# Causal attention: queries made and turned by heads, the first pairs before the last queries, VectorE's row work ahead of the inversion

## What is computed

```python
q = (x @ Wq).reshape(b, t, H, D)                  # H = 16 heads, D = 64: 32 plain, 32 to be turned
ckv = x @ Wkva                                    # 16 latent columns, 32 key columns to be turned
kv_latent, k_rope = ckv[:, :, :R], ckv[:, :, R:]
q = concat([q_nope, rope(q_rope)]); k = concat([kv, rope(k_rope)]); v = concat([kv, 0])
att = softmax(where(tril, q @ k.T / sqrt(D), -inf))   # 512 x 512, causal
y = (att @ v) @ Wo
```

## Time and profile before

| | us |
|---|---|
| median of three runs | 1535.96 (1533.09 to 1536.89) |
| the profiled execution | 1537.09 |
| its span, first to last instruction | 1535.1 |
| TensorE busy in the span | 1282.3 (84%) |
| VectorE, ScalarE, GpSimd busy | 949.6, 718.9, 531.6 |
| the causal attention in the span | 818.6 to 1172.3 |
| its exponentials of the first unit | at 849.1 |

### The profile page before, as it was taken

One profiled execution on the slowest core, in us unless ns is written; L12 is line 12 of the kernel. 1 busy time (PEld: TensorE's weight loads), 2 busy tenths in 40 slices (PEclk: granted clock), 3 DMA queues, 4 the chain that ended last, 5 costly groups with the idle time before them and its releaser, 6 DMA issues. The chain is left out here.

```text
span 1535.1 us, 25211 instructions
## 1 busy us (share of the span) xinstructions
PE 1282.3 (84%) x8930; PEld 743.7 (48%) x8930; DVE 949.6 (62%) x2159; ACT 718.9 (47%) x1936; POOL 531.6 (35%) x625
## 2 busy tenths in 40 slices
PE   3799718879999969958995889898987968987998
PEld 2444306745565636644433556564654434443443
DVE  6466631255756764566655788888664855665764
ACT  3254503367666524434442665656673333453222
POOL 2320250445433544341002565657452320001443
PEclk8599959989999979968996999999997986998999
DMA  2355021151000013230000000000000010000000
GB/s 57 108 168 128 25 69 39 41 119 15 1 1 1 8 60 108 56 65 9 11 2 1 1 1 1 1 1 1 1 1 1 1 22 13 10 3 1 7 7 14
DMA packets 67134, 45.31 MB, mean 30 GB/s; under 512 B 17707, under 2 KB 60403, under 8 KB 67011
## 3 DMA queue, kind: packets, MB, share of 16 engines
q1 hardware_dynamic: 61155, 34.48, 8.8%
q0 software_dynamic: 4096, 8.40, 2.3%
q10 hardware_dynamic: 1760, 0.82, 0.3%
HBM read 24.91 MB, written 13.89 MB: 25 GB/s over the span
## 5 line engine op out<-in xcount | busy, mean ns | idle before, releaser
L3479 ACT ACTIVATE L2a_pr<-psum,L2a_negmax 128x512 f32<-128x512 f32 (+3 forms) x256 | 132.2, 531 | 94.8 <-DVE L2a_negmax L3605 40.2
L585 ACT ACTIVATE L1x_praw<-psum,L1x_negmax 128x154 f32<-128x154 f32 x256 | 96.1, 390 | 56.9 <-DVE L1x_negmax L710 56.8
L3344 PE MATMUL psum<-ident,L2a_pr 128*128 128x128 f32 x640 | 86.6, 280 | 20.3 <-DVE L2a_pT L3618 12.9
L319 POOL TENSOR_TENSOR L1x_pm<-L1x_praw,L1x_total 128x1024 f32<-128x1024 f32 x32 | 60.8, 1899 | 122.3 <-DVE L1x_total L716 104.5
L3344 PEld LDWEIGHTS psum<-ident,L2a_pr 128*128 128x128 f32 x640 | 72.4, 144 | 25.9 <-issue 23.4
L2041 POOL TENSOR_TENSOR L3f_scaled<-L3f_sg,L3f_wide 128x512 f32<-128x512 f32 (+1 forms) x44 | 55.8, 1272 | 66.8 <-ACT L3f_sg L2120 37.8
L1674 DVE TENSOR_REDUCE L3x_negmax<-psum 128x6 f32<-128x924 f32 (+1 forms) x48 | 47.7, 1011 | 46.7 <-PE psum L1212 37.4
L1674 DVE TENSOR_REDUCE L0x_negmax<-psum 128x6 f32<-128x924 f32 (+1 forms) x48 | 47.8, 1011 | 45.5 <-PE psum L1212 41.0
L3232 POOL TENSOR_TENSOR L2a_pr<-L2a_pr,L2a_total 128x768 f32<-128x768 f32 x32 | 48.7, 1522 | 69.7 <-DVE L2a_total L3634 69.5
L3229 POOL TENSOR_TENSOR L2a_pr<-L2a_pr,L2a_total 128x1024 f32<-128x1024 f32 x29 | 56.5, 1950 | 46.0 <-DVE L2a_total L3634 45.9
L710 DVE TENSOR_REDUCE L1x_negmax<-psum 128x4 f32<-128x616 f32 x64 | 50.7, 793 | 31.4 <-PE psum L390 28.3
(11 more groups left out here) (744 smaller groups left out, 3335.5 us busy)
## 6 DMA issues: line engine op xcount, KB each, us to landing
expert_arena<-in_L_ffn_w SPq DMA_DIRECT2D x16, 256.0 KB, 4.4
group_in<-zero SPq DMA_DIRECT2D x2, 1472.0 KB, 9.3
L1f_xs<-group_in SPq DMA_DIRECT2D x10, 256.0 KB, 4.0
group_out<-L1f_ys SPq DMA_DIRECT2D x10, 256.0 KB, 2.4
L1f_gu<-in_L_ffn_gate_up_w SPq DMA_DIRECT2D x8, 256.0 KB, 3.7
slots_in<-zero SPq DMA_DIRECT2D x1, 1280.0 KB, 9.4
L0f_xs<-slots_in SPq DMA_DIRECT2D x5, 256.0 KB, 4.0
resid<-in_x SPq DMA_DIRECT2D x4, 256.0 KB, 5.9
```

What stands on the lines that cost most here:

```text
L319: nc.gpsimd.tensor_tensor(pm[:, n % 2].rearrange("p j t k -> p (j t) k"), praw[:, n % 3, :, :, 0:MAIN].rearrange("p j t k -> p (j t) k"), ...
L585: nc.scalar.activation(praw[:, n % 3, j, t, :], psum[:, 2 * u + j, x * CTX:(x + 1) * CTX], ACT.Exp, bias=negmax[:, n % 2, u, j, x:x + 1], ...
L3344: last = nc.tensor.transpose(psum[:, TURN + n // 4, n % 4 * P:(n % 4 + 1) * P], pr[:, m % RING, n * P:(n + 1) * P], core.ident[:])
L3479: ins = nc.scalar.activation(pr[:, i % RING, SEQ * j + lo:SEQ * j + hi], psum[:, bank + j, lo:hi], ACT.Exp, bias=negmax[:, i % RING, e:e + ...
```

## The change

- The query products go by head half: x = 2 to 5 are the row tiles 0 to 3 of heads 0 to 7, then x = 6 transposes the keys, 7, 8, 11 and 12 make heads 8 to 15, 9 and 10 transpose pairs 0 and 1, 13 is the gap, 14 to 19 transpose pairs 2 to 7.
- A piece to turn is two row tiles of eight heads, again 512, 256, 256 and 512 elements. Pairs 0 to 3 wait for pieces 0 and 1, pair 4 for pieces 2 and 3. The cosines are stored twice side by side (`cos2`, two GpSimd copies ahead of the loop).
- GpSimd turns pieces 0 and 2, started at x = 4 and 9; VectorE pieces 1 and 3, at x = 6, 7 and 13, 14. Ahead of the loop VectorE turns pieces 0 and 1, GpSimd piece 2; VectorE turns piece 3 at steps 2 and 3.
- `AHEAD` is 11 instead of 14. Ten fronts (0 to 9) run ahead of the loop; step 0 issues fronts 10 and 11, step i then front 11 + i. All events of a batch's fronts, turns and `normalised` by ScalarE come at other steps with it (units 14 and 19 of a batch instead of 10 and 14).
- VectorE's `inverted(i - 1)` moves from behind `turned` to the end of the step, behind all row work.
- ScalarE's copy of the front moves ahead of `normalised`.
- The routing's transposes, logits and choice in the last batch come one step later.

The diff, cut; the indices and waits that follow from the above are left out:

```diff
-    AHEAD = 14
+    AHEAD = 11
-    POOL_TURNS, VEC_TURNS = {3: 0, 7: 2}, {6: (1, 0), 7: (1, 1), 10: (3, 0), 11: (3, 1)}
+    KEYS, GAP = 6, 13
+    QUERIES = {2: (0, 0), 3: (1, 0), 4: (2, 0), 5: (3, 0), 7: (0, 1), 8: (1, 1), 11: (2, 1), 12: (3, 1)}
+    PAIRS = {9: 0, 10: 1, 14: 2, 15: 3, 16: 4, 17: 5, 18: 6, 19: 7}
+    DUE = [3, 5, 8, 12]
+    POOL_TURNS, VEC_TURNS = {4: 0, 9: 2}, {6: (1, 0), 7: (1, 1), 13: (3, 0), 14: (3, 1)}
...
+    def fronts(i):
+        return [k for k in (range(AHEAD - 1, AHEAD + 1) if i == 0 else (AHEAD + i,)) if k < B * FRONT]
...
-        def turn_queries(on, v, tmp, t, parts=(0, 1)):
+        def turn_queries(on, v, tmp, piece, parts=(0, 1)):
-            x = qpad[:, t, :, 0:ROPE]
+            t0, h0 = 2 * (piece % 2), 8 * (piece // 2)
+            x = qpad[:, t0:t0 + 2, h0:h0 + 8, 0:ROPE]
+            cos = cos2[:, t0:t0 + 2, :].unsqueeze(2).to_broadcast([P, 2, 8, ROPE])
...
-                pool.wait_ge(s["fr"], count(10))
-                turn_queries(nc.gpsimd, v, rope_g, QT - 1).then_inc(s["qp"], 1)
+                pool.wait_ge(s["fr"], count(DUE[2]) + 1)
+                turn_queries(nc.gpsimd, v, rope_g, 2).then_inc(s["qp"], 1)
...
                         if g == 0:
-                            pe.wait_ge(s["qd"], QT - 1 + 2 * f)
-                            pe.wait_ge(s["qp"], 1 + 2 * f)
+                            pe.wait_ge(s["qd"], 2 * f + 2)
+                            if f:
+                                pe.wait_ge(s["qp"], 2 * f)
+                        if g == 4:
+                            pe.wait_ge(s["qd"], 2 * f + 3)
+                            pe.wait_ge(s["qp"], 2 * f + 1)
...
                     if i < N:
                         exps(i)
+                    for k in fronts(i):
+                        front(k)
                     if i - 1 in by_act:
                         normalised(i - 1)
-                    if AHEAD + i < B * FRONT:
-                        front(AHEAD + i)
...
-                for t in range(QT - 1):
-                    dve.wait_ge(s["fr"], 2 + 2 * (t + 1))
-                    turn_queries(nc.vector, v, rope_d, t).then_inc(s["qd"], 1)
+                for piece in range(2):
+                    dve.wait_ge(s["fr"], count(DUE[piece]) + 1)
+                    turn_queries(nc.vector, v, rope_d, piece).then_inc(s["qd"], 1)
...
                     if 0 <= i - LAG < N:
                         turned(i - LAG)
-                    if 0 <= i - 1 < N:
-                        inverted(i - 1)
...
                     if b >= 0 and part < 4:
                         finished(b, part)
+                    if 0 <= i - 1 < N:
+                        inverted(i - 1)
```

More of the change, by code:

```diff
@@ L3163, in causal_attention @@
         stats_v, stats_s = rows_rstd(core, L, s["var"], s["sd"])
-        def turn_queries(on, v, tmp, t, parts=(0, 1)):
+        def turn_queries(on, v, tmp, piece, parts=(0, 1)):
             half = ROPE // 2
-            x = qpad[:, t, :, 0:ROPE]
[L3169 to L3172, removed]
+            t0, h0 = 2 * (piece % 2), 8 * (piece // 2)
+            x = qpad[:, t0:t0 + 2, h0:h0 + 8, 0:ROPE]
+            same, other = (tmp[:, n].rearrange("p (t h) e -> p t h e", t=2) for n in range(2))
+            cos = cos2[:, t0:t0 + 2, :].unsqueeze(2).to_broadcast([P, 2, 8, ROPE])
+            up = w["sin"][:, t0:t0 + 2, :].unsqueeze(2).to_broadcast([P, 2, 8, half])
+            down = nsin[:, t0:t0 + 2, :].unsqueeze(2).to_broadcast([P, 2, 8, half])
             if 0 in parts:
-                v.step(on.tensor_tensor(tmp[:, 0].rearrange("p h (a e) -> p h a e", a=2), pairs, cos, ALU.mult))
-                v.step(on.tensor_tensor(tmp[:, 1, :, 0:half], x[:, :, half:ROPE], down, ALU.mult))
+                v.step(on.tensor_tensor(same, x, cos, ALU.mult))
+                v.step(on.tensor_tensor(other[:, :, :, 0:half], x[:, :, :, half:ROPE], down, ALU.mult))
             if 1 in parts:
-                v.step(on.tensor_tensor(tmp[:, 1, :, half:ROPE], x[:, :, 0:half], up, ALU.mult))
+                v.step(on.tensor_tensor(other[:, :, :, half:ROPE], x[:, :, :, 0:half], up, ALU.mult))
                 v.done()
-                return on.tensor_tensor(x, tmp[:, 0], tmp[:, 1], ALU.add)
+                return on.tensor_tensor(x, same, other, ALU.add)
         def turn_keys(on, v, tmp, f):
@@ L3210, in _ @@
                 nc.gpsimd.tensor_scalar(nsin[:], w["sin"][:], -1.0, None, ALU.mult).then_inc(s["const"], 1)
-                pool.wait_ge(s["const"], 5)
+                for a in range(2):
+                    nc.gpsimd.tensor_scalar(cos2[:, :, ROPE // 2 * a:ROPE // 2 * (a + 1)], w["cos"][:], 1.0, None, ALU.mult).then_inc(s["const"], 1)
+                pool.wait_ge(s["const"], 7)
                 nc.gpsimd.affine_select(out=future[:], in_=future[:], compare_op=ALU.is_ge, fill=-1e30, base=0,
@@ L3391, in _ @@
                 last.then_inc(s["wo_ps"], 1)
-                pe.wait_ge(s["const"], 6)
-                for k in range(AHEAD):
-                    if k == 9:
+                pe.wait_ge(s["const"], 8)
+                for k in range(AHEAD - 1):
+                    if front_bank(k) == 6:
                         pe.wait_ge(s["wvo"], 1)
@@ L3457, in front @@
                     else:
-                        g = x - 12
+                        g = PAIRS[x]
                         if f:
@@ L3527, in _ @@
                         exps(i)
+                    for k in fronts(i):
+                        front(k)
                     if i - 1 in by_act:
                         normalised(i - 1)
-                    if AHEAD + i < B * FRONT:
-                        front(AHEAD + i)
                     if i == NEXT + 2:
                         router.spread_root(act)
-                    if i == NEXT + 8:
+                    if i == NEXT + 9:
                         router.rows_out(act, 0, router.xnT[:], IN)
```

61 lines of the change are left out of this document (32 added, 29 removed).

## The result

The changed kernel takes **1511.95 us** (median of four runs, 1507.21 to 1516.27), the kernel before, in the same comparison, 1535.87. The ratio is 0.985, 95% interval 0.9821 to 0.9878: 24 us faster, where 17 were forecast. 1511.95 lies inside the range of 1508 to 1531. The profiled execution took 1516.27 us (span 1514.3).

What follows compares the result with a forecast made beforehand. TensorE sets the pace, with about 7 us of waits a batch. Profiled 1537.1 - 4.4 (start) - 9.8 (loop) - 2.8 (end) = 1520.1; the median is 1.1 lower, so 1519 us, range 1508 to 1531.

Steps and rivals of the forecast that it cites:

- The fourth rival: Steps 15, 16, 22 to 28: GpSimd still multiplies when row work comes; slower, 1548 us or, by half, 1541; chance 0.08.
- rival 2: Loop: everything hides, TensorE runs near its own work, 7.5 us less a batch; 1506 us; chance 0.13.
- The start: Before the loop and its first steps: earlier scores and lost waits, less new waits; -4.4 us, between -1 and -6.
- its two bounds: First pair's start: 838.2 if VectorE's last step runs free (taken), 839.3 if GpSimd's piece gets in front.
- The -0.95 us for scores at full clock: First scores: TensorE comes from an idle time under 1 us, so they run 0.95 us shorter.
- The new wait for front 11: Step 0: front 11 waits until ScalarE has copied front 10 from the same bank; TensorE idles 2.9 us.
- The loop: Three middle batches: 7.75 us go and 4.5 come in each, net -3.25 a batch, -9.8 us in all.
- What was to go: Each loop batch: waits of 1.21, 0.68, 1.93, 1.16 and 1.27 us and 1.5 us of low clock, together 7.75.
- steps 15 and 16: Each batch: GpSimd turns only two steps ahead of VectorE's half turn; 2.4 us of TensorE waits, bounded by 1.2 and 3.3.
- steps 22 to 28: Each batch: last turn, normalising and finishing of the batch before fall together; TensorE waits 0.5 and 1.1, 1.6 us.
- The end: Last batch: three waits go (-7.1), 2.5 us of waits stay, three more fronts cost 1.8; -2.8 us.
- -1.21 - 0.68 us a batch: Loop: TensorE's waits for front copies standing behind ScalarE's scaling go when the copy comes first.

Runs made afterwards that it cites:

- split_only: The changed kernel with the inversion and ScalarE's scaling both back in their old places, leaving the split by heads: 1537.43 us.
- inv_back: The changed kernel with VectorE's inversion put back ahead of the row work: 1532.78 us.
- act_back: The changed kernel with ScalarE's scaling of a unit put back ahead of the front's copy: 1526.25 us.
- bank: The changed kernel with front 10 in a bank of its own, so front 11 waits for nothing at step 0: 1503.8 us.
- pool_early: The changed kernel with GpSimd's first piece turned one step earlier in each batch: 1506.03 us.
- pool_late: The changed kernel with GpSimd's piece before the loop held until VectorE has turned its two: 1510.08 us.
- orders_only: The kernel before with the inversion behind the row work and ScalarE's front copy ahead of its scaling, without the split by heads: 1499.32 us.
- act_only: The kernel before with only ScalarE's front copy moved ahead of its scaling: 1536.29 us.
- inv_only: The kernel before with only the inversion moved behind the row work: 1506.58 us.
- hybrid: The kernel before with both orders, split by heads for batch 0 only, GpSimd's two pieces held for VectorE's two, first loop front in its own bank: 1494.4 us.

## Why the prediction was right, and where it was not

**Right in its main step.** Row work beside a multiply was named as what makes VectorE late, and the move of the inversion as what parts them, with a margin of 0.3 us. With the inversion put back the whole gain is gone, with the move alone all of it is there. The fourth rival (the multiply still runs when the row work comes) didn't come about: no normalising step of the three batches is slowed. The time itself, 1512, is at the lower edge of the forecast's own range (1512 to 1526), about halfway to rival 2, in which everything hides (1506): of the 4.5 us a batch that were to come, 3.1 came.

**The start, -4.4 forecast, -2.6 measured.** The scores start 4.8 us earlier after the key product (11.87 against 16.67) instead of 5.8: the meeting of GpSimd's piece with VectorE's last step happened, and I had taken the wrong one of its two bounds, "because the two start together". GpSimd's piece started 0.4 us ahead of that step, and so, by 0.2 to 0.5 us, in the four other traces with the same start and the meeting (split_only, inv_back, act_back, bank); in pool_early it started 0.26 us behind. Only there was the bound that I took right: one trace of six. The -0.95 us for scores at full clock was wrong in the profiled execution: after a wait of 2.83 us they took 2.08 us, and the products of steps 0 and 1 stayed slow (1.65 for unit 1's scores against 0.92). Where the meeting didn't slow VectorE the wait was 1.65 us (pool_late) or 1.26 (pool_early) and they took 1.13: the one term hung on the other. The new wait for front 11 was sized well (2.9 forecast, 2.54), that for the steps after it too high (3.0 forecast, 1.18 + 0.61 = 1.8). That the start gained at all was in part luck: the sum put it down to the early pair, but the inversion alone, without any early pair, gives 2.1 us (45.59 against 47.72, orders_only 45.39), with the waits of 0.20 and 1.39 us at steps 4 and 5 gone, and the split alone loses 4.2.

**The loop, -9.8 forecast for three batches, -17.8 measured.** What was to go went. What was to come was priced too high: steps 15 and 16 at 2.4 us (1.41 + 0.40 = 1.8), step 20 at 0.5 (nothing), steps 22 to 28 at 1.6 (0.28 + 0.79 + 0.47 = 1.5, at steps 23, 27 and 28; a wait of 0.28 us stood at step 27 before already and shouldn't have counted). That is 4.5 against 3.1 us, for three batches 4 us. Another 3.5 us of the 17.8 are the routing's first wait, 2.62 us with its slow transposes, which the cut puts into the third stretch and the prediction into the end.

**The end, -2.8 forecast.** The stretches from step 69 on gained 4.3 us, with the 3.5 above 7.8. The three waits of 2.62, 1.69 and 1.94 us went, and 2.5 us were to stay; TensorE's waits from step 60 to 75 are now 0.32, 0.37 and 0.53. The four products take 1.14 us, as estimated (1.3), and no transposes wait for them. The 2.5 us were a guess without a row.

**Wrong: what each part is worth.** The sum put -1.21 - 0.68 us a batch down to ScalarE's order and -4.4 us to the split, as if waits were worth their length. Alone, ScalarE's order is worth nothing (act_only), because TensorE then only waits longer for VectorE (at steps 15 and 18); on top of the inversion it is worth 4.1 us of the stage, and with the split 17.0. The split costs 8.4 us of the stage when both orders are there (320.15 against 311.71): 2.1 us a batch, 6.2 in three, from the collision at step 15 and the waits at steps 22 to 28, and 2.75 us in the last stretch, which is the clock there, while up to step 9 it gains 0.3. Its early pair was paid back in the first steps: by the front 11 that waits in the same bank (3.1 to 3.8 us), and by the collision with GpSimd (up to 1.7 with the clock, which chance alone can give too). The prediction had all these as costs in its sum; what it didn't see is that the kernel without the split doesn't need to pay them.

**The rest.** Everything ahead of the stage took 3.7 us longer in the profiled execution of after than in that of before (the key product starts at 832.39 instead of 828.65), where the two kernels are the same. So the profiled times differ by 20.8 us and the medians by 23.9.

## What to carry to other kernels

Two engines that slow each other can be parted by the order of the instruction that releases one of them: the reciprocal was moved behind the row work of its step and gave 28 us by the medians (inv_only), since GpSimd's multiply then runs beside VectorE's work from PSUM. Waits of a chain of engines are not priced by their lengths: take one away, and ask which wait of the same step stands behind it; here that one gave a part 0 us or 17 depending on the others. And a change made of parts should be run part by part: one of three gave the gain, one took some of it back.

## What the runs showed of the hardware

Where VectorE and GpSimd both run a chain of steps on tiles in SBUF, both get slower, step by step: in the trace with ScalarE's order put back, at 893.5 us, VectorE's 512 elements took 1.27 instead of 0.69 us and its 256 took 0.94 instead of 0.42, nearly GpSimd's own step of 1.28; in the changed kernel GpSimd's steps of 256 took 1.17 and 0.90 us in the same place, where they take 0.72 when alone. So VectorE's half turn cost 1.1 us more there, not the 1.9 of a whole multiply. The Trainium skill, "SBUF — State Buffer", section Who interferes with whom, has such steps with two inputs in SBUF contend with GpSimd's reads; the rows agree, and read as if in a chain the two engines took turns, step by step.

The clock after a wait was not a constant of the kernel: the first scores took 1.13 us where the pair before them waited 0.50 us (hybrid), 1.26 (pool_early) or 1.65 (pool_late), and 2.08 where it waited 2.83 (after), though after and pool_early run the same instructions up to there; the last value products, the same in both kernels, took 4.50 us in the trace of after and 2.36 in that of the inversion alone.
